# Two-expert feed-forward with cross attention: tiles turned in 16-bit halves, per-group statistics moved to GpSimd, new instruction orders

## The chip, the cores and the metric

The kernel runs on one core of one Trainium2 chip. The metric is the device time of one execution in microseconds, the median of several. A core has five engines that work side by side, each through its own instruction list in order: TensorE (PE, with weight loads shown as PEld), VectorE (DVE), ScalarE (ACT), GpSimd (POOL) and SyncE (SP), which only issues transfers here. They wait for one another through semaphores.

## What is computed

`x` and `ctx_1024` hold 128 sequences of 64 tokens with 128 features, all in float32. Cut to what matters, the reference is:

```python
def attn(query, kv):                       # causal, one head, per sequence
    scores = einsum('bqd,bkd->bqk', query, kv) * 128 ** -0.5
    scores = where(tril, scores, -inf)
    return einsum('bqk,bkd->bqd', softmax(scores), kv)

x = x + attn(layernorm(x), ctx_1024)
xt = layernorm(x).reshape(-1, 128)         # 8192 tokens
logits = xt @ gate_w.T                     # 8 experts
_, idx = top_k(logits + beta, 2)
c = zeros(B, 8).at[rows, idx].add(sigmoid(logits[idx]))
h = silu(xt @ gate_proj[e]) * (xt @ up_proj[e])     # every expert e, width 256
combined = sum_e c[:, e] * (h @ down_proj[e])
shared = (silu(xt @ shared_gate) * (xt @ shared_up)) @ shared_down
x = x + combined + shared
```

## The kernel before

**Two stages.** The first takes the 8192 tokens in 16 groups of 512 (`G = 16`, four tokens to each of the 128 partitions, `GT = 4`). It does the attention, the routing and the shared expert, writes `x + attention + shared` to the output, and scatters each token's normalised row (128 features, token number, two expert numbers, two weights: `ROW = 133` float32) to a place in the DRAM array `sorted_rows` that depends on its pair of experts. The second stage reads this array back in 91 tiles of 128 rows (64 regular ones, and 27 with what the lists left over, which are taken two at a time), so 78 steps (`PAIRS`) of one or two tiles; a step multiplies its tiles with the two experts' weights and adds the result to the output through an indirect DMA.

**A group in the first stage.** VectorE takes mean and variance of the incoming tokens (`statistics(g, 0)`, line 873) and, from the attention's result, of the second layer norm (`statistics(g, 1)`). Both share one small computation for index j (first norm of group j, second of group j - 3; `LEAD = 3`): VectorE adds epsilon (`variances`, line 902), GpSimd raises to the power -1/2 (`powers`, line 441), and VectorE multiplies mean and result to a shift (`shifts`, line 907). The first norm itself is written by GpSimd for two of the four tokens (`normalise_x`, line 448; VectorE's `normalise_first` does it for the first four groups) and by ScalarE for the other two (`shift_x`, line 668). TensorE turns the result (line 1433), ScalarE copies it, TensorE adds mask and scores (lines 1440 and 1448), VectorE takes the row maximum (`row_max`, line 915), ScalarE the exponentials, TensorE the attention (`attend`, line 1473), VectorE the residual (`residual`, line 930). Then `normalise` on ScalarE (line 659), `transpose_xn2` (line 1485), `route` (line 1493) and `turn_logits` (line 1499) on TensorE, `bias_logits` and `choose` on VectorE (lines 941 to 974: the two experts and a one-hot row `chosen` of the pair), `pick` on GpSimd (line 465: the logits' tanh at the chosen experts), `weights` on VectorE (line 983), `ranks` on TensorE (lines 1508 to 1514: the token's place in its pair's list) and `slots` on VectorE (lines 988 to 995), and at last four indirect DMAs of `scatter` on GpSimd (line 478). The shared expert is `shared_gate_mm` and `shared_up_mm` (lines 1527 and 1536, 512 columns each), `silu_gates`, `hidden` (line 1002), `shared_down_mm` (line 1548) and `sum_up` (line 1008).

**Order.** All five lists are written out by hand: a prologue, a loop over pairs of groups, and an epilogue. Each engine obeys its own list, so an instruction that waits holds everything behind it. SP loads `x` into a ring of five buffers (`RX = 5`): `load_x(5)` is the first that waits, for `residual(0)`, and it stands behind the 2.1 MB that fill `sorted_rows` with padding and behind `load_c(4)` and `load_c(5)`.

**From the first stage to the second.** `tile_table` and `slot_tables` on VectorE (lines 1030 to 1066) work out where each tile lies and which experts it needs; TensorE's `list_ends` and `spread_table` (lines 1555 and 1560) stand in its list between the last shared matrix products. After `shared_down_mm(15)` TensorE does eight products that keep it busy (line 1822), and then turns the first tiles.

**A step of the second stage** is in TensorE's list: `gate_up(i)` (line 1609; 8 products of 128x128x128 in float32, which the profile shows as 16 instructions), `transpose_tile(i + 2)` (line 1575, one instruction for each tile, into PSUM bank G0 or U0), `tile_down(i - 1)` (line 1633, 8 instructions). VectorE's list for it: `tile_hidden(i)` (line 1171), `copy_tile_T(i + 2)` (line 1121, from PSUM to SBUF), `tile_weights(i + 1)`, `tile_out(i - 1)`; in steps 0 to 7 the tables for the left-over rows (`left_table`, `extra_table`) come on top.

## Time and profile before

| | |
|---|---|
| median of 3 runs | 396.43 us (396.29 to 396.6) |
| the profiled execution, its own time | 396.57 us |
| its span | 394.9 us |
| TensorE busy | 379.7 us, 96% |
| VectorE busy | 294.4 us, 75% |
| ScalarE busy | 236.2 us, 60% |
| GpSimd busy | 251.0 us, 64% |
| first matrix product of the second stage | at 169.98 us |

The profiled execution's own time is 0.14 us over the median, and 1.67 us longer than its span. Times of the trace count from the span's start. Matrix instructions are pipelined, so the busy time of a short stretch of TensorE contains their overlap; the distance from one start to the next tells what each costs. The granted clock was 0.996 of full speed over the span.

### The profile page before, as it was taken

The numbers are of one execution on the slowest core, as the hardware profiler recorded it, in microseconds if no ns is written. First come the engines' busy times: TensorE is split into PE (matmuls) and PEld (weight loads), VectorE is DVE, ScalarE is ACT, GpSimd is POOL, SyncE is SP. The second block draws the span as 40 slices with busy tenths as digits, with TensorE's granted clock in tenths as the row PEclk, the third lists the DMA queues.
The fourth block names the chain that finished last, engine by engine and source line by source line (L and its number), as shares of the span: only waits on it lengthen the run. The fifth ranks groups of instructions, "written<-read, shape, count | busy, mean of one in ns | idle before, by whom it ended". The sixth has DMA issues, their size and how long they took to land.

```text
span 394.9 us, 11090 instructions
## 1 busy us (share of the span) xinstructions
PE 379.7 (96%) x3321; PEld 318.3 (81%) x3321; DVE 294.4 (75%) x1308; ACT 236.2 (60%) x558; POOL 251.0 (64%) x275
## 2 busy tenths in 40 slices
PE   8979999999999999899999999999999999999993
PEld 3445666666666665689999999999999999999993
DVE  4988989999998896687966666667677666666662
ACT  2689898798888863355566565652211565656540
POOL 6636888888877787338787788886100045645464
PEclk9999999999999999999999999999999999999998
DMA  7953464896442112247556775554332113332223
GB/s 239 354 165 103 141 210 136 253 280 199 136 149 83 64 62 77 70 120 143 104 86 91 87 100 77 72 81 59 59 74 55 36 21 54 45 48 23 26 22 27
DMA packets 43049, 41.78 MB, mean 106 GB/s; under 512 B 5688, under 2 KB 31808, under 8 KB 42992
## 3 DMA queue, kind: packets, MB, share of 16 engines
q1 hardware_dynamic: 30864, 30.69, 26.8%
q0 software_dynamic: 12128, 10.40, 19.1%
q8 instruction: 28, 0.46, 0.5%
q14 instruction: 29, 0.24, 0.2%
HBM read 24.17 MB, written 16.90 MB: 104 GB/s over the span
## 4 chain that ended last, share of the span: by engine, by line
PE 57%; POOL 1%; issue 1%; DVE 1%; ACT 0%; POOLq 0%; DVEq 0%
PE gu_pair L1609 35%; PE bank L1633 17%; PE bank L1575 2%; PE bank L1548 1%; POOL out L529 1%; PE bank L1536 0%; PE gu_pair L1822 0%; POOL sorted_rows L478 0%; PE bank L1527 0%; DVE acc L1008 0%; PE gu_pair L1560 0%; DVE hid L1002 0%; ACT tile_T L727 0%; DVE t_out L1211 0%; DVE t_part L1205 0%
## 5 line engine op out<-in xcount | busy, mean ns | idle before, releaser
L529 POOL DMA_INDIRECT out<-t_out,tile_in x64 | 100.2, 1565 | 85.0 <-DVE t_out L1211 70.6
L1609 PE MATMUL gu_pair<-tile_T,W_slot 128*128 128x128 f32 x1024 | 124.8, 275 | 0.5 <-ACT tile_T L727 0.5
L1609 PEld LDWEIGHTS gu_pair<-tile_T,W_slot 128*128 128x128 f32 x1024 | 119.5, 192 | 0.7 <-issue 0.7
L756 ACT ACTIVATE t_silu<-gu_pair 128x512 f32<-128x512 f32 (+1 forms) x78 | 46.4, 594 | 101.8 <-PE gu_pair L1609 94.8
L1171 DVE SCALAR_TENSOR_TENSOR t_hid<-t_silu,gu_pair 128x512 f32<-128x512 f32 (+1 forms) x78 | 53.1, 680 | 48.4 <-PE gu_pair L1609 47.2
L1633 PE MATMUL bank<-W_down,t_hid 128*128 (+1 forms) x620 | 82.3, 276 | 0.1
L478 POOL DMA_INDIRECT sorted_rows<-rows,slot x64 | 63.4, 990 | 20.5 <-issue 20.0
L1633 PEld LDWEIGHTS bank<-W_down,t_hid 128*128 128x128 f32 x620 | 75.4, 192 | 0.7 <-issue 0.7
L746 ACT ACTIVATE W_slot<-W 128x512 f32 x128 | 73.2, 622 | 3.9 <-DVE slot_pair L1062 2.0
L489 POOL DMA_INDIRECT left_in<-sorted_rows,left_index x27 | 26.1, 967 | 16.8 <-DVE left_index L1089 8.9
L441 POOL TENSOR_TENSOR rstd<-var_eps,minus_half 128x8 f32<-128x8 f32 (+1 forms) x19 | 27.9, 1470 | 10.9 <-DVE var_eps L902 10.5
L1536 PE MATMUL bank<-xn_T,shared_gu 128*128 128x512 f32 x64 | 33.9, 611 | 0.6 <-ACT silu_g L723 0.6
L1548 PEld LDWEIGHTS bank<-shared_dn,hid 128*128 128x128 f32 x256 | 29.9, 192 | 5.0 <-issue 4.5
L1548 PE MATMUL bank<-shared_dn,hid 128*128 128x128 f32 x256 | 31.9, 278 | 1.5 <-issue 0.9
L1527 PE MATMUL bank<-xn_T,shared_gu 128*128 128x512 f32 x64 | 33.0, 603 | 0.0
L659 ACT ACTIVATE rows<-x,shift,rstd 128x128 f32<-128x128 f32 x64 | 26.3, 485 | 3.4 <-DVE shift L907 3.3
L1609 PE MATMUL gu_pair<-tile_T,W 128*128 128x128 f32 x216 | 26.4, 275 | 0.0
L1609 PEld LDWEIGHTS gu_pair<-tile_T,W 128*128 128x128 f32 x216 | 25.2, 192 | 0.0
L1211 DVE SCALAR_TENSOR_TENSOR t_out<-bank,t_weight,t_part 128x128 f32<-128x128 f32 x64 | 22.5, 351 | 2.3
L1121 DVE COPY tile_T<-bank 128x128 f32<-128x128 f32 (+1 forms) x76 | 23.3, 306 | 0.0
L1002 DVE TENSOR_TENSOR hid<-silu_g,bank 128x512 f32<-128x512 f32 x32 | 21.6, 677 | 2.2 <-ACT silu_g L723 1.6
L1575 PE MATMUL bank<-ident,tile_in 128*128 128x128 f32 x91 | 22.5, 273 | 0.0
(158 smaller groups left out, 543.5 us busy)
## 6 DMA issues: line engine op xcount, KB each, us to landing
tile_in<-sorted_rows SPq DMA_DIRECT2D x91, 66.5 KB, 2.0
x_sb<-x SPq DMA_DIRECT2D x16, 256.0 KB, 4.4
c_T<-ctx_cols SPq DMA_DIRECT2D x16, 256.0 KB, 3.1
c_sb<-ctx SPq DMA_DIRECT2D x16, 256.0 KB, 4.6
out<-acc SPq DMA_DIRECT2D x16, 256.0 KB
sorted_rows<-padding SPq DMA_DIRECT2D x1, 2128.0 KB, 12.7
sorted_rows<-left_in SPq DMA_DIRECT2D x27, 66.5 KB, 2.4
sorted_rows<-rows,slot POOLq DMA_INDIRECT x64, 3.1
```

The source lines that it names most:

```text
L441: e.tensor_tensor(rstd[:, j % 2, n], var_eps[:, n], minus_half[:, n], ALU.pow).then_inc(s_rstd, 1)
L478: e.indirect_dma_start(sorted_rows, bass.IndirectOffsetOnAxis(ap=slot[:, g % RR, i:i + 1], axis=0), rows[:, g % RR, i, :], None).then_inc( ...
L529: e.indirect_dma_start(out_flat, bass.IndirectOffsetOnAxis(ap=tile_in[:, tiles_of(i)[0] % NR, ID:ID + 1].bitcast(I32), axis=0), t_out[:, q ...
L746: r = e.activation(W_slot[:, q % TX, h], W[:, bass.ds(experts[q][h] * WN, WN)], ACT.Copy)
L756: e.activation(t_silu[:, 0:n * M], gate_up_pair[i % 2][0][:, 0:n * M], ACT.Silu).then_inc(s_t_silu, 1)
L1171: e.scalar_tensor_tensor(out=t_hid[:, i % 2, 0:n * M], in0=t_silu[:, 0:n * M], scalar=0.5, in1=gate_up_pair[i % 2][1][:, 0:n * M], op0=ALU ...
L1527: e.matmul((G0, G1)[m], shared_gu[:, 0, m * P:(m + 1) * P], xn2_T[:, g % RT], start=True, stop=True).then_inc(s_gate[m], 1)
L1536: e.matmul((U0, G0)[m], shared_gu[:, 1, m * P:(m + 1) * P], xn2_T[:, g % RT], start=True, stop=True).then_inc(s_up[m], 1)
L1548: r = e.matmul(Y[:, i * D:(i + 1) * D], hid[:, g % 2, m, i * P:(i + 1) * P], shared_dn[:, m], start=(m == 0), stop=(m == MC - 1), skip_gro ...
L1575: r = e.transpose(tile_pair[i % 2][:, h * P:(h + 1) * P], tile_in[:, n % NR, 0:D], ident[:])
L1609: r = e.matmul(bank[:, c:c + P], w, tile_T[:, i % TX, tile], start=True, stop=True, skip_group_check=True)
L1633: r = e.matmul(y, t_hid[:, i % 2, c:c + P], w, start=(m == 0), stop=(m == MC - 1), skip_group_check=True)
```

## The change

It has six parts.

1. From step 2 of the second stage on, each tile is turned as two matrices of 16-bit numbers: the low and the high halves of the float32 words, each read with a step of two 16-bit elements, each turned against a bfloat16 identity. `copy_tile_T` then puts the halves together again, as 16-bit integers, 256 of them for each tile in place of 128 float32.
2. `variances` and `shifts` go from VectorE to GpSimd; there the negated mean is a separate instruction.
3. From group 4 on GpSimd normalises one token in four, and ScalarE three.
4. `scatter` is split in two halves, which stand apart in GpSimd's list.
5. `pick` for groups 13 to 15 is done by VectorE (`pick_late`).
6. The lists of all five engines get a new order.

```diff
@@ sync_program
             load_x(0)
-            load_c(0)
             load_x(1)
             e.dma_start(router[:], gate_w).then_inc(s_router_in, 16)
+            load_c(0)
+            load_x(2)
             load_c(1)
-            load_x(2)
+            load_x(3)
             e.dma_start(beta_all[:], ...
             load_c(2)
-            load_x(3)
@@ gpsimd_program
+            def variances(j):
+                n = norms(j)
+                if j < G:
+                    e.wait_ge(s_moments[0], j + 1)
+                if j >= LEAD:
+                    e.wait_ge(s_moments[1], j - LEAD + 1)
+                if j:
+                    e.wait_ge(s_shift, j)
+                    e.wait_ge(s_rstd, j)
+                e.tensor_scalar(minus_mean[:, n], moments[:, j % 2, n, :, 0], -1.0, None, ALU.mult).then_inc(s_minus_mean, 1)
+                e.tensor_scalar(var_eps[:, n], moments[:, j % 2, n, :, 1], EPS, None, ALU.add).then_inc(s_var_eps, 1)
...
+            def shifts(j):
+                n = norms(j)
+                e.wait_ge(s_minus_mean, j + 1)
+                e.wait_ge(s_rstd, j + 1)
+                e.tensor_tensor(shift[:, j % 2, n], minus_mean[:, n], rstd[:, j % 2, n], ALU.mult).then_inc(s_shift, 1)
...
-                for i in range(GT // 2):
-                    r = e.tensor_scalar(xn[:, i], x_sb[:, g % RX, i], moments[:, g % 2, 0, i, 0:1],
-                                        rstd[:, g % 2, 0, i:i + 1], ALU.subtract, ALU.mult)
-                r.then_inc(s_normal[0], 1)
+                e.tensor_scalar(xn[:, 0], x_sb[:, g % RX, 0], moments[:, g % 2, 0, 0, 0:1],
+                                rstd[:, g % 2, 0, 0:1], ALU.subtract, ALU.mult).then_inc(s_normal[0], 1)
...
-                for i in range(GT):
+                for i in range(half * GT // 2, (half + 1) * GT // 2):
                     e.indirect_dma_start(
                         sorted_rows, bass.IndirectOffsetOnAxis(ap=slot[:, g % RR, i:i + 1], axis=0),
@@ scalar_program, shift_x
-                for i in range(GT // 2, GT):
+                for i in range(GT // 2 if g < FIRST else 1, GT):
@@ vector_program
+            def pick_late(g):
+                e.wait_ge(s_is_chosen, g + 1)
+                e.wait_ge(s_tanh, g + 1)
+                e.wait_ge(s_weights, g)
+                e.tensor_tensor(picked[:, :, :, 0:E], is_chosen[:, :, :, :],
+                                tanh_l[:, :, :].rearrange("p t (a e) -> p t a e", a=1).broadcast_to([P, GT, K, E]),
+                                ALU.mult).then_inc(s_picked, 1)
@@ copy_tile_T
-                e.tensor_copy(tile_T[:, i % TX, 0:n].rearrange("p h n -> p (h n)"), tile_pair[i % 2][:, 0:n * P]).then_inc(s_tile_T, 1)
+                e.tensor_copy(tile_T[:, i % TX, 0:n].bitcast(U16).rearrange("p h (n c) -> p h c n", c=2),
+                              tile_halves[i % 2][:, 0:n * 2 * P].bitcast(U16).rearrange("p (h c n) -> p h c n", h=n, c=2)
+                              ).then_inc(s_tile_T, 1)
@@ vector_program, the part of its order between residual(1) and residual(2)
             residual(1)
             statistics(1, 1)
-            variances(4)
-            pair_tables()
             row_max(2)
             normalise_first(3)
-            shifts(4)
+            statistics(5, 0)
+            inverse_sums(2)
             bias_logits(0)
             choose(0)
-            statistics(5, 0)
             slots(0)
             weights(0)
-            inverse_sums(2)
             row_max(3)
             residual(2)
@@ vector_program, its order from choose(14) on
             choose(14)
+            pick_late(14)
+            weights(14)
             sum_up(12)
+            slots(14)
+            hidden(13, 1)
             hidden(13, 0)
-            slots(14)
-            weights(14)
-            hidden(13, 1)
             bias_logits(15)
             choose(15)
+            pick_late(15)
+            weights(15)
             slots(15)
             hidden(14, 0)
-            weights(15)
-            sum_up(13)
             hidden(14, 1)
             tile_table()
-            sum_up(14)
+            sum_up(13)
             hidden(15, 0)
             slot_tables()
+            sum_up(14)
             hidden(15, 1)
@@ transpose_tile
-                    r = e.transpose(tile_pair[i % 2][:, h * P:(h + 1) * P], tile_in[:, n % NR, 0:D], ident[:])
+                    if i < 2:
+                        r = e.transpose(tile_pair[i][:, 0:P], tile_in[:, n % NR, 0:D], ident[:])
+                        continue
+
+                    halves = tile_in[:, n % NR, 0:D].bitcast(BF16).rearrange("p (d c) -> p d c", c=2)
+                    for c in range(2):
+                        r = e.transpose(tile_halves[i % 2][:, (2 * h + c) * P:(2 * h + c + 1) * P], halves[:, :, c], ident_bf[:])
@@ tensor_program, its order from transpose_probs(2) to attend(2)
-            shared_gate_mm(0, 1)
+            shared_gate_mm(0, 0)
             turn_logits(0)
             transpose_probs(2)
             transpose_xn(3)
+            shared_gate_mm(0, 1)
+            transpose_xn2(1)
             ranks(0)
-            transpose_xn2(1)
             mask_scores(3)
             score(3)
             attend(2)
@@ tensor_program, its order from ranks(15) on
             ranks(15)
+            shared_up_mm(14, 1)
+            list_ends()
             shared_down_mm(13)
-            shared_up_mm(14, 1)
+            shared_up_mm(15, 0)
+            shared_gate_mm(15, 0)
             shared_gate_mm(15, 1)
-            list_ends()
+            spread_table()
             shared_down_mm(14)
-            shared_gate_mm(15, 0)
-            shared_up_mm(15, 0)
-            spread_table()
             shared_up_mm(15, 1)
             shared_down_mm(15)
```

The new lists for the groups between are of the same kind: the same calls, in another order.

## Rows read from the trace of the kernel before

**Rows 1.** Busy time by stretch: stretch, length, then each engine's busy us (instructions)

```profile
80.00:100.00 20.00, 20.00 (x203) 13.14 (x202) 19.08 (x103) 17.29 (x49) 17.10 (x21) 1.00 0.73 225
190.00:200.00 10.00, 9.98 (x87) 9.56 (x86) 8.92 (x26) 6.17 (x12) 7.89 (x7) 1.00 0.46 92
250.00:280.00 30.00, 30.00 (x272) 30.00 (x271) 19.77 (x63) 12.95 (x24) 21.95 (x15) 1.00 0.51 67
```

**Rows 2.** Chain that ended last, second stage: start us, length us, what

```profile
253.50 1.78 PE gu_pair L1609 x16
255.28 0.11 PE bank L1575
255.39 0.89 PE bank L1633 x8
```

**Rows 3.** Timeline of PE, one group of the first stage: start us, us, what

```profile
86.81 1.02 PE L1536 MATMUL bank<-xn_T,shared_gu 128*128 128x512 f32 x2
87.67 0.21 PE L1508 MATMUL gu_pair<-chosen,before_bf 128*128 128x112 bf16 x1
87.72 0.24 PE L1511 MATMUL gu_pair<-chosen,steps_bf 128*128 128x84 bf16 x3
87.81 0.46 PE L1514 MATMUL gu_pair<-list_next,last_row 128*128 128x112 f32 x2
88.11 0.27 PE L1440 MATMUL gu_pair<-mask,ident_bf 128*128 128x256 bf16 x1
88.22 1.02 PE L1527 MATMUL bank<-xn_T,shared_gu 128*128 128x512 f32 x2
89.17 0.67 PE L1473 MATMUL gu_pair<-c_sb,probs_T 64*64 64x128 f32 x16
```

**Rows 4.** Groups by line and shape: count, busy us, mean ns, idle before

```profile
L1609 PEld LDWEIGHTS gu_pair<-tile_T,W_slot 128*128 128x128 f32 x1024 | 119.5, 192 | 0.7 <-issue 0.7
L1121 DVE COPY tile_T<-bank 128x128 f32<-128x128 f32 x63 | 17.9, 283 | 0.0
L1121 DVE COPY tile_T<-bank 128x256 f32<-128x256 f32 x13 | 5.4, 418 | 0.0
L902 DVE TENSOR_SCALAR var_eps<-moments 128x8 f32<-128x8 f32 x13 | 2.7, 205 | 0.7
L907 DVE SCALAR_TENSOR_TENSOR shift<-moments,rstd 128x8 f32<-128x8 f32 x13 | 2.1, 162 | 0.7 <-POOL rstd L441 0.6
L448 POOL TENSOR_SCALAR xn<-x_sb,moments,rstd 128x128 f32<-128x128 f32 x24 | 18.9, 791 | 1.1 <-PE gu_pair L1433 0.3 <-POOL rstd L441 0.2
```

**Rows 5.** Timeline of DVE, prologue, and chosen of groups 2 and 11

```profile
23.34 0.19 DVE L941 TENSOR_TENSOR biased<-gu_pair,beta_all 128x32 f32<-128x32 f32 x1
25.07 0.27 DVE L974 TENSOR_TENSOR chosen<-pair_code,code 128x112 bf16<-128x112 f32 x1
26.55 0.87 DVE L873 BATCH_NORM_STATS2 stats<-x_sb 128x6 f32<-128x128 f32 x4 [1.21 <-DMA x_sb<-x]
...
42.36 0.27 DVE L974 TENSOR_TENSOR chosen<-pair_code,code 128x112 bf16<-128x112 f32 x1
...
123.44 0.27 DVE L974 TENSOR_TENSOR chosen<-pair_code,code 128x112 bf16<-128x112 f32 x1
```

**Rows 6.** Timeline of SP, prologue: issue of x, group 5; page, median to landing

```profile
19.01 0.43 SPq L323 DMA_DIRECT2D x_sb<-x  x1
...
x_sb<-x SPq DMA_DIRECT2D x16, 256.0 KB, 4.4
```

**Rows 7.** Timeline of the end of the first stage, all engines

```profile
154.18 0.27 DVE L974 TENSOR_TENSOR chosen<-pair_code,code 128x112 bf16<-128x112 f32 x1
157.52 0.33 POOL L465 TENSOR_TENSOR picked<-is_chosen,tanh_l 128x64 f32<-128x64 f32 x1
157.88 0.23 DVE L983 TENSOR_REDUCE rows<-picked 128x8 f32<-128x72 f32 x1 [1.47 <-POOL picked L465]
165.55 2.02 PE L1548 MATMUL bank<-shared_dn,hid 128*128 128x128 f32 x16 [0.88 <-issue]
```

598 lines of the change are left out of this document (353 added, 245 removed).

## Prediction

> **What bounds the kernel now.** I read the chain that ended last first. In the second stage it is TensorE alone: a step is 16 instructions of gate and up, one turned tile, 8 instructions of down, and the next step starts where the last one ends [rows 2]. 1.78 us for 16 and 0.89 us for 8 is 0.111 us each; a turned tile costs 0.11 us, the same. So whatever changes a step on TensorE changes the time, some 76 times over, and what VectorE does is beside the path as long as it keeps its lead. The busy time by stretch shows that lead: between 250 and 280 us VectorE is busy for 19.77 us of 30, TensorE for all of it [rows 1].
>
> For the first stage the busy table shows TensorE at 20.0 us of 20 and VectorE at 19.08 [rows 1], but a short product's busy time contains its neighbours, so I take starts. From choosing group 2 to choosing group 11, 42.36 to 123.44 us, nine groups take 9.0 us each [rows 5]. What a group costs TensorE I add up from start to start in the timeline [rows 3]: a pair of 512-column instructions 0.86 (86.81 to 87.67), four pairs 3.4; ranks 0.44 (87.67 to 88.11); attention some 0.6, and as much for the scores, which are as many instructions; the 16 instructions of down 1.78, as for 16 of gate and up [rows 2]; turning both norms, the probabilities and the logits eleven times 0.11; routing and mask, two short runs, some 0.5. The sum is about 8.6 us (3.4 + 0.4 + 1.2 + 1.8 + 1.2 + 0.5). VectorE's share of 19.08 in 20 is 8.6 us of a 9.0 us group. So both engines are within 0.4 us of the period, and neither can be relieved by more than that without the other being late next.
>
> **Tiles in halves, on TensorE.** 76 of the 78 steps change. A tile's one instruction of 0.11 us goes. In its place come two bfloat16 instructions of 128 columns. The nearest row is the 112-column bfloat16 product, which hands over after 0.05 us (87.67 to 87.72) [rows 3]; for 128 columns that is 0.056, and two make 0.112. The streaming is a wash. What is not a wash is the weight load behind them. A float32 load takes 192 ns from start to end and comes at TensorE's pace of 0.111 us [rows 2, 4], hidden because a product just as long runs ahead of it. In the changed step the first float32 load of the down product has only 0.056 us of bfloat16 work to hide in. The trace has this case once a group: two float32 products of 112 columns behind a bfloat16 product of 28 columns take 0.30 us, 87.81 to 88.11, where two at the steady pace take 0.22 [rows 3]. That is 0.08 us lost behind a product of some 0.03 us. Where the product ahead is as long as the load (0.11 us) nothing is lost. Between the two, at 0.056, the loss is 0.05 on a line and 0.04 if the load has a fixed length; I take 0.045. It comes once a step, with one tile or two: 76 x 0.045 = **+3.4 us**, bounds 0 and 76 x 0.08 = 6.1.
>
> The trace shows no weight load with a step between elements. If it doesn't get the short bfloat16 load but moves at the pace of the float32 load, each half costs 0.11: then 62 steps of one tile gain 0.11 us and 14 steps of two tiles 0.22, together 6.8 + 3.1 = +9.9 us. I take the short load as likelier, because the bfloat16 products of the ranks hand over in 0.05 us and less [rows 3], so a bfloat16 load is no brake there. The lower end is that nothing is lost; below that I see no way, since streaming alone is already even.
>
> A rule of the Trainium skill speaks against this part too: "TensorE: Matmul & The Clock Gate", section "Back-to-back issue gap", puts a stream of load-and-product pairs at about 81 ns each for 128 columns. The rows here disagree for short bfloat16 products (0.05 us and less [rows 3]). By the page two halves would take 0.162 us in place of 0.111, which is 89 tiles x 0.05 = +4.5 us, an estimate from that page.
>
> **Putting the halves together, on VectorE.** One tile's copy goes from 128 to 256 elements, read from PSUM and written with a step; the row of 256 elements is 418 ns against 283 [rows 4]. That is +0.135 us in 62 steps, and by the same slope +0.27 us in 14 steps: 12 us of VectorE. It lies beside TensorE's work: a step of 2.79 us has about 0.95 us of VectorE idle (10.2 of 30 us [rows 1]). Only while the tables for the left-over rows are made is the cover thin: 8.92 of 10 us busy between 190 and 200 us [rows 1]. Some seven steps there, each 0.135 longer, against 1.1 us idle in 10: I add 0.3 us, bounds 0 and 1. If the cover were gone everywhere, it would be up to 12 us, but the idle time is three to seven times the addition.
>
> Second stage: 3.4 + 0.3 = **+3.7 us**.
>
> **Prologue.** This is an order that can be read. VectorE's new list has `statistics(5, 0)` ahead of `bias_logits(0)` and `choose(0)`; before, it stood behind. In the trace choosing ran from 23.34 to 25.34 us, and only then did VectorE wait, until 26.55 us, for x of group 5 [rows 5]. That load was issued at 19.01 us [rows 6], behind the padding, c of group 4 and c of group 5, which the change leaves ahead of it. It took 7.5 us, 19.01 to 26.55, where the median load of x takes 4.4 [rows 6], so it hangs on the bytes ahead, and an earlier issue would not help much. I keep its landing near 26.5. Then VectorE does the statistics (1.25 us), and choosing (2.0 us) begins near 27.9 and ends near 29.9, 4.6 us later than before. Queued behind it: `slots(0)`, `row_max(3)`, `residual(2)`; on TensorE `ranks(0)` with the scores of group 3 and attention of group 2 behind. Since VectorE only swapped two items of 1.25 and 2.0 us around a wait, what it is late by afterwards is the 2.0 us of choosing that it could have done before the landing: **+2.2 us** with the small operations. Bounds: 0, if x lands by 23.3, and 4.6.
>
> **Steady groups.** `variances` and `shifts` leave VectorE: 0.205 + 0.162 = 0.37 us for each group [rows 4]. GpSimd gains three small instructions for them. Its nearest prices are 0.33 us for 64 elements on each of 128 partitions [rows 7] as an upper end, and nothing beyond issue as a lower, so 0.3 to 1.0 us; it loses one normalised token of 0.79 [rows 4]. It was busy for 17.10 of 20 us [rows 1] and stays about there. ScalarE gains that token: by its own share of 17.29 in 20 it has 1.2 us idle in a group, and the token takes it about half a microsecond. Both stay off the path, but ScalarE now runs near 90%. The gain on the path is not 0.37: TensorE's sum of 8.6 allows at most 0.4 before it is the one that is late, and both engines would need perfect order. I take half, 0.2 us for each of 11 groups: **-2.2 us**, bounds 0 and -4.4.
>
> **Scatters by halves** change no count; their only customers are the ring of seven row buffers and the second stage's start, so I cost them at nothing.
>
> **End of the first stage.** Before, VectorE waited 1.47 us for GpSimd's pick of group 15, which stood behind scatters [rows 7]. `pick_late` takes that wait away, for three instructions of at most 0.33 us [rows 7]. What is late next is TensorE's own list. From the end of choosing group 15 (154.45) to `shared_down_mm(15)` at 165.55 are 11.1 us [rows 7]. In the new order `slot_tables` still stands behind `hidden(15, 0)`, which needs both gate products of group 15 and their silu, and `hidden(15, 1)` behind that. So the chain from choosing on keeps its members; only the picking leaves it, and other products now come between. I take **-0.3 us**; the bounds are +1, the three instructions on VectorE with nothing hidden, and -2, the wait and a little more.
>
> **Sum.** 396.57 (the profiled execution) + 3.7 + 2.2 - 2.2 - 0.3 = 400.0 us. That execution is 0.14 us over the median of the runs, so 399.8.
>
> **Rivals.** First, *the new orders fill TensorE's gaps*. It has 9.0 against 8.6 us in each group, and more in the prologue. If the orders win back 4 us over the groups, 1.5 us at the end, and x of group 5 lands before VectorE asks for it, the sum is 396.4 + 3.7 - 5.5 = 394.6, faster. It decides from 4.5 us won in the first stage on. For it: VectorE's relief is real, 0.37 us a group. Against: 8.6 us leaves no room for more, and the swap above. 0.18.
>
> Second, *turning in halves costs nothing*, because the first float32 load is hidden some other way: 399.8 - 3.4 = 396.4, no change. For it: the streaming is even. Against: the 0.30 us of two float32 products [rows 3]. 0.14.
>
> Third, *the stepped load is slow*: 399.8 - 3.4 + 9.9 = 406.3. For it: no such load in the trace. 0.12.
>
> Fourth, *the prologue's loss is not won back*, since ScalarE at 90% or GpSimd's longer chain (mean, variance, power, shift, between scatters) holds the groups at 9.0 us: 399.8 + 2.2 = 402.0. 0.14.
>
> The forecast has 0.42 and its own range 398 to 401.5.
>
> **How the numbers follow.** A measurement of this kernel tells about 0.2% (0.8 us) from no change. Faster by more: 0.14 of the first rival, 0.05 of the second, 0.01 of the forecast, and some for a mix of the first two: 0.23. Within 0.2%: 0.04 of the first, 0.09 of the second, 0.01: 0.14. Slower: 0.63. The range for 8 in 10 leaves out a third of the first rival below, half of the third above: 394.0 to 406.0.
>
> **What would show it.** In the chain after: the distance from the end of gate and up to the down product, 0.11 before, should be about 0.11 with the down product's 8 instructions taking 0.93 to 0.95 in place of 0.89, so a step of 2.83 us; 2.79 means the second rival, 2.9 the third. VectorE's wait for x of group 5 should stand ahead of choosing group 0, at about 26.5 us, and choosing end near 30. The period of groups 2 to 11 should be 8.8 us; at 8.65 the first rival is at work, at 9.0 the fourth. The first product of the second stage should start near 169.7 us (169.98 before). The prediction is wrong if the turned halves take another time than the rows of bfloat16 products give, or if x of group 5 comes early.

## The result: 23 us slower, and where they are

The changed kernel takes 419.86 us (median of 4 runs, 419.59 to 420.61), the kernel before, run beside it, 396.51 (396.29 to 396.92). The ratio is 1.0591 (1.0572 to 1.0609), so +23.4 us where 3.3 were forecast. The profiled execution took 420.07 us with a span of 418.3.

Where the time lies can be read from a few starts that both traces have: the one-hot row `chosen` of groups 0, 2, 11 and 15, and the first product of the second stage. Before, they stand at 25.07, 42.36 and 123.44 [rows 5], 154.18 [rows 7] and 169.98. After, first in the timeline of DVE (start us, us, what):

```profile
26.78 0.87 DVE L988 BATCH_NORM_STATS2 stats<-x_sb 128x6 f32<-128x128 f32 x4 [4.63 <-DMA x_sb<-x]
...
29.75 0.27 DVE L1073 TENSOR_TENSOR chosen<-pair_code,code 128x112 bf16<-128x112 f32 x1
...
45.94 0.27 DVE L1073 TENSOR_TENSOR chosen<-pair_code,code 128x112 bf16<-128x112 f32 x1
...
138.09 0.27 DVE L1073 TENSOR_TENSOR chosen<-pair_code,code 128x112 bf16<-128x112 f32 x1
...
172.36 0.27 DVE L1073 TENSOR_TENSOR chosen<-pair_code,code 128x112 bf16<-128x112 f32 x1
172.72 0.23 DVE L1083 TENSOR_TENSOR picked<-is_chosen,tanh_l 128x64 f32<-128x64 f32 x1
```

and in that of PE:

```profile
187.38 1.80 PE L1722 MATMUL gu_pair<-tile_T,W_slot 128*128 128x128 f32 x14 [0.46 <-ACT tile_T L806]
```

| stretch | before | after | difference | forecast |
|---|---|---|---|---|
| start to `chosen` of group 2 | 42.36 | 45.94 | +3.6 | +2.2 |
| group 2 to group 11 | 81.08 (9.0 a group) | 92.15 (10.2) | +11.1 | -1.8 (8.8) |
| group 11 to group 15 | 30.74 | 34.27 | +3.5 | -0.4 |
| group 15 to the second stage | 15.80 | 15.02 | -0.8 | -0.3 |
| second stage | 224.9 | 230.9 | +6.0 | +3.7 |

The fourth column adds up to 23.4. Most of it is in the groups, where the forecast had a small gain. There TensorE and VectorE are no longer nearly full, as the busy time by stretch shows (columns as in [rows 1], whose first row had TensorE at 20.00 and VectorE at 19.08):

```profile
80.00:100.00 20.00, 18.97 (x175) 12.15 (x177) 17.35 (x95) 16.40 (x47) 15.48 (x23) 1.00 0.79 251
100.00:120.00 20.00, 17.50 (x158) 11.26 (x150) 14.58 (x86) 16.10 (x47) 15.00 (x23) 1.00 0.50 149
120.00:140.00 20.00, 18.81 (x169) 12.99 (x170) 17.32 (x99) 15.76 (x46) 13.50 (x21) 0.91 0.31 97
```

So they wait. For what, the table of waits says (engine and line, what it waited for: us in total, times, longest). Before:

```profile
PEld gu_pair L1508 <- DVE chosen L974: 6.3, 13, 0.8
DVE stats L873 <- DMA x_sb<-x: 3.6, 2, 2.4
ACT rows L659 <- DVE shift L907: 3.3, 7, 1.1
```

After:

```profile
DVE stats L988 <- DMA x_sb<-x: 17.9, 9, 4.6
PEld gu_pair L1615 <- DVE chosen L1073: 13.7, 12, 3.8
ACT rows L738 <- POOL shift L464: 11.3, 11, 1.5
```

Two waits at the head of a chain are new in size: VectorE for x, 17.9 us where it was 3.6, and ScalarE for a shift, 11.3 where it was 3.3. (TensorE's wait for `chosen`, 13.7 where it was 6.3, follows from the first: in the next section it falls to 5.2 as soon as x is on time.) The first has its reason in two lists read side by side. SP's queue and VectorE, after, at group 8 (start us, us, what):

```profile
51.38 0.33 SPq L333 DMA_DIRECT2D c_T<-ctx_cols  x1
51.75 1.00 SPq L334 DMA_DIRECT2D c_sb<-ctx  x1
52.79 0.44 SPq L328 DMA_DIRECT2D x_sb<-x  x1
```

```profile
53.51 0.38 DVE L996 BATCH_NORM_AGGREGATE moments<-stats 128x2 f32<-128x6 f32 x4
57.67 0.87 DVE L988 BATCH_NORM_STATS2 stats<-x_sb 128x6 f32<-128x128 f32 x4 [3.78 <-DMA x_sb<-x]
...
60.57 0.27 DVE L1073 TENSOR_TENSOR chosen<-pair_code,code 128x112 bf16<-128x112 f32 x1
```

SP holds `load_x(8)` behind `load_c(8)`, and `load_c(8)` waits for group 4's attention, since c has a ring of four buffers (`RC = 4`). The new list of VectorE has `statistics(8, 0)` directly behind `residual(4)` and `statistics(4, 1)`, so VectorE asks for x of group 8 at 53.9 us, 1.1 us after its transfer was issued, and the transfer takes more than 4. VectorE sits idle for 3.78 us, with `choose(3)` queued behind. Before, the same statistics stood behind `residual(5)`, one group later, and its x had been issued 9.5 us earlier:

```profile
47.92 0.43 SPq L323 DMA_DIRECT2D x_sb<-x  x1
...
57.39 0.86 DVE L873 BATCH_NORM_STATS2 stats<-x_sb 128x6 f32<-128x128 f32 x4
```

So the new list asks for x four groups ahead of the residual where the old one, in its loop, asked three ahead, and SP's list, which is the same in its loop, lets x of four groups ahead start only about when that residual does. In the loop `statistics(g + 9, 0)` stands likewise behind `residual(g + 5)`, with `statistics(g + 5, 1)` and `row_max(g + 6)` between. Of the 17.9 us of such waits 9.9 are in the groups, six waits of 0.4 to 3.8 us (x of groups 6, 8, 11, 13, 14 and 15); before, there was none in the groups, and all 3.6 us were in the prologue.

### The profile page after: what moved, and what is told of

Read it like the earlier page. It is cut to its first block, busy times and chain, and to the rows that moved or that the text cites. A ratio compares the mean times of both kernels' runs of the same rounds, so it can differ in the third digit from the quotient of the medians.

```text
span 418.3 us, 11327 instructions
## 1 busy us (share of the span) xinstructions
PE 389.2 (93%) x3414; PEld 325.3 (78%) x3414; DVE 303.8 (73%) x1273; ACT 240.6 (58%) x570; POOL 255.8 (61%) x317
## 4 chain that ended last, share of the span: by engine, by line
PE 54%; DVE 4%; POOL 2%; issue 2%; ACT 1%; DVEq 0%; POOLq 0%; ACTq 0%
PE gu_pair L1722 30%; PE bank L1746 16%; PE bank L1688 2%; PE bank L1655 2%; PE bank L1634 1%; POOL sorted_rows L499 1%; PE bank L1643 1%; DVE extra_sum L1286 1%; ACT rows L738 1%; POOL out L550 1%; DVE t_hid L1281 1%; DVE tile_T L1229 1%; PE gu_pair L1964 0%; DVE t_out L1321 0%; DVE t_part L1313 0%
## 5 line engine op out<-in xcount | busy, mean ns | idle before, releaser
L1746 PE MATMUL bank<-W_down,t_hid 128*128 (+1 forms) x620 | 86.3, 282 | 1.5 <-DVE t_hid L1281 1.3
L499 POOL DMA_INDIRECT sorted_rows<-rows,slot x64 | 64.7, 1010 | 24.6 <-issue 21.8
L1229 DVE COPY tile_T<-bank 128x256 uint16<-128x256 uint16 (+1 forms) x76 | 37.2, 490 | 0.0
L738 ACT ACTIVATE rows<-x,shift,rstd 128x128 f32<-128x128 f32 x64 | 26.3, 484 | 11.3 <-POOL shift L464 11.3
L988 DVE BATCH_NORM_STATS2 stats<-x_sb 128x6 f32<-128x128 f32 x64 | 13.9, 280 | 18.0 <-DMA x_sb<-x 17.9
```

Of the source, the lines that this page charges most:

```text
L499: e.indirect_dma_start(sorted_rows, bass.IndirectOffsetOnAxis(ap=slot[:, g % RR, i:i + 1], axis=0), rows[:, g % RR, i, :], None).then_inc( ...
L738: r = e.activation(rows[:, g % RR, i, 0:D], x2[:, g % RG, i], ACT.Identity, bias=shift[:, (g + LEAD) % 2, 1, i:i + 1], scale=rstd[:, (g + ...
L1229: e.tensor_copy(tile_T[:, i % TX, 0:n].bitcast(U16).rearrange("p h (n c) -> p h c n", c=2), tile_halves[i % 2][:, 0:n * 2 * P].bitcast(U16 ...
L1746: r = e.matmul(y, t_hid[:, i % 2, c:c + P], w, start=(m == 0), stop=(m == MC - 1), skip_group_check=True)
```

## Experiments

All are runs of whole kernels, each compared with the kernel before on the same chip (medians 396.3 to 397.4 us, with one exception, which is named). Starts and waits of a kernel come from its one profiled execution. Where a difference between two kernels is given, it is the difference of their ratios times 396.5.

### Late x: mended in the changed kernel, and made in the kernel before

**x ahead of c** (changed kernel). Theory: the late x is most of the loss.

```diff
             for it in range(2, G + 3):
-                if it + 3 < G:
-                    load_c(it + 3)
                 if it + 3 < G:
                     load_x(it + 3)
+                if it + 3 < G:
+                    load_c(it + 3)
```

> The changed kernel with one edit: in SP's loop the load of x for a group stands ahead of the load of c for it, so it waits only for the residual five groups back and no longer for the attention four groups back. In the changed kernel VectorE waits 17.9 us in total for x, nine times, and the nine groups from choosing group 2 to choosing group 11 take 10.2 us each. Theory (late x): the waits for x from group 6 on vanish, the period falls to 9.2 us or less and the time to about 409 us (419.9 less 11). Rival (GpSimd's chain of mean, variance, power and shift holds the groups, and VectorE would wait for something else): the waits for x vanish too, but the period stays above 10 us and the time above 417 us. Second rival (the lower granted clock of TensorE in three stretches is the cause and not a result): time above 417 us and the clock still falls.

Measured: 411.03 us, ratio 1.0371 (1.0346 to 1.0396). That is 8.7 us less than the changed kernel. The waits for x fall from 17.9 to 7.4 us, three in the prologue, the longest of them, 3.9, for group 5; in the groups none is left.

Groups 2 to 11 go from 10.2 to 9.3 us each (`chosen` at 45.16 and 128.87), not to 9.0.

**x one turn later** (kernel before). The opposite test: nothing of the change but a late x.

```diff
-                if it + 3 < G:
-                    load_x(it + 3)
+                if it == 2:
+                    load_x(5)
+                if 6 <= it + 2 < G:
+                    load_x(it + 2)
```

> The kernel before with one edit: from group 6 on SP issues the load of x one turn of its loop later, so behind the load of c of the next group. This gives the kernel before the distance of the changed one: the load is issued after the attention whose residual stands just ahead of the statistics that read it. Theory (late x is what lengthens the period): VectorE waits some 2 us for x in each group, the period grows from 9.0 to about 10.5 us and the time to about 410 us. Rival (VectorE's wait is filled from slack and the period is set elsewhere): at most 399 us.

Measured: 431.53 us, 1.0891 (1.0857 to 1.0926), +35 us, far more than expected. VectorE's waits for x:

```profile
DVE stats L875 <- DMA x_sb<-x: 32.9, 12, 6.8
```

29.3 us more of waiting (32.9 against 3.6) cost 35 us, and in the run above 10.5 us less gave back 8.7. Part of the 35 is TensorE's clock: granted at 0.967 over the span where the kernel before has 0.996, which is at most some 13 us. That leaves 22 to 35 us for the 29.3. So a wait of VectorE ahead of choosing costs most of its length or all of it: little of it is covered by other work, and the chain through choosing sets the period.

**x ahead of c in the kernel before**, the same diff as the first, on a kernel whose VectorE waits only 3.6 us for x.

> The kernel before with one swap on SP's list: in the loop x of a group is loaded ahead of its c. Its VectorE waited only 3.6 us for x, twice. If a late x costs what it waits, 2 to 3 us less: 394 (393 to 395.5). If the old order has room to hide it, no change: 396.4. A loss would mean that the c that is now later is what attention waits for.

Measured: 395.64 us, 0.9969 (0.9959 to 0.998), -1.2 us. The swap moves the issue of `load_x(5)` from 19.0 to 15.5 us, and the waits for x go from 3.6 to 2.0. The traces don't show that the gain comes from there: the kernel with halves alone (below) has SP's old order, waits 2.4 us for x in its profiled execution and chooses group 15 at 153.42 us, and this one at 153.46. The expected 2 to 3 us would have needed the whole wait gone.

### The prologue

**statistics(5, 0) behind choosing**, on top of x ahead of c (changed kernel).

```diff
-            statistics(5, 0)
             inverse_sums(2)
             bias_logits(0)
             choose(0)
+            statistics(5, 0)
```

It ran first, with three of the kernels of the next sections, at a time when the kernel before itself took 459.7 us, for a reason that the runs don't show. The ratios of then (0.9641 for this one; 0.995, 1.0057 and 1.0103 for part 2, part 3 and part 5 alone) are used for nothing, and all four were run again beside a kernel before of 397.4 us.

> The changed kernel with x ahead of c in SP's loop, as in the run e1_x_ahead_of_c (411.0 us), and also the statistics of group 5 behind choosing group 0, as before. In e1 VectorE still waits 3.9 us at once for x of group 5 and chooses group 0 at 29.0 us (25.1 in the kernel before). Theory (that wait holds choosing, and what it costs is what VectorE could have done before the landing, 2.0 us): choosing group 0 ends near 26 us, choosing group 2 comes near 43 us in place of 45.2, and the time is 409 us. Rival (the delay is given back later anyway, since other chains hold the groups): 411 us, no change.

> The kernel of e5_x_ahead_stats_behind again, since in that job the kernel before took 459.7 us in place of 396.5 and everything waited longer. The changed kernel with x ahead of c in SP's loop and the statistics of group 5 behind choosing group 0. Theory (the wait for x of group 5 costs the 2 us of choosing that could be done before): 409 us where e1_x_ahead_of_c took 411.0. Rival (given back later by other chains): 411 us.

Measured: 408.04 us, 1.028 (1.0258 to 1.0301), 3.6 us less than with x ahead of c alone by the ratios, 3.0 by the times. `chosen` of group 0 starts at 26.04 in place of 28.97, and the 3 us stay with it to the end. The wait itself explains these 2.9 us. With it went a stretch of low clock: from 28 to 36 us the granted clock was 0.58 with the wait, and the mean of the span rose from 0.989 to 0.995, so some of the 3.6 can be clock. Groups 2 to 11 still take 9.3 us each.

### Turned halves

**Float32 turns in the changed kernel** and **halves alone in the kernel before**: part 1 taken out of the one and put into the other (the two hunks of `copy_tile_T` and `transpose_tile` of the diff above, backwards and forwards).

> The changed kernel with its tiles turned and copied as float32, as before; all else of the change stays. The step of the second stage is 2.79 us again in place of 2.845, and the stalls near 200 us and between 310 and 340 us go. Theory (each step loses one float32 weight load behind a short product, 0.055 us, 76 times, and VectorE's longer copies 1.8 us): 419.9 - 6 = 413.9 us. Rival (the copies cost nothing of their own; the 1.8 us come from the new order): 419.9 - 4.2 = 415.7 us. Rival (the halves cost nothing): 419.9 us.

> The kernel before with only part 1 of the change: tiles from step 2 on turned in halves and copied as 16-bit integers. Theory (0.055 us of TensorE a step, 76 steps, and 1.8 us of stalls behind VectorE's copies): 396.5 + 6 = 402.5 us. Rival (only TensorE's part): 400.7 us. The forecast's own size for this part was 3.7 us: 400.2 us.

Measured: without the halves 413.57 us, 1.0433 (1.0407 to 1.0458), so they cost 6.3 us of the change; alone 402.55 us, 1.0159 (1.0133 to 1.0185), +6.3 us. The two agree, and a third pair below gives 6.1. This part stands by itself. Its costs are seen in the chain of the second stage, after (start us, length us, what; before [rows 2]):

```profile
252.95 1.79 PE gu_pair L1722 x16
254.74 0.11 PE bank L1688 x2
254.85 0.95 PE bank L1746 x8
```

and in the groups by shape (count, busy us, mean ns; before [rows 4]):

```profile
L1688 PEld LDWEIGHTS bank<-ident_bf,tile_in 128*128 128x128 bf16 x178 | 16.5, 99 | 0.8
L1229 DVE COPY tile_T<-bank 128x256 uint16<-128x256 uint16 x63 | 27.7, 440 | 0.0
L1229 DVE COPY tile_T<-bank 128x512 uint16<-128x512 uint16 x13 | 9.5, 729 | 0.0
```

Two halves take the 0.11 us of the one tile; the down product behind them takes 0.95 in place of 0.89. With finer digits the first float32 product of down starts 0.056 us after the second half, and the next one 0.165 after it, 0.055 over the pace of 0.111: 76 x 0.055 = 4.2 us. Of the other 1.8 us, 1.1 lie in one place. In the chain after:

```profile
325.53 1.79 PE gu_pair L1722 x16
327.31 0.13 PE bank L1688 x2
327.44 0.71 DVE tile_T L1229
...
330.05 0.45 DVE tile_T L1229
...
332.79 0.69 DVE t_hid L1281
...
333.52 1.16 PE bank L1746 x8
```

From 327 to 333 us the chain leaves TensorE and runs over VectorE. These are the last steps with two tiles, where VectorE has the copy of 512 elements (0.73 us, 0.42 before) and a row of `extra_sum` instructions that wait for one another. TensorE is idle for 1.1 us of 300 to 340 (38.91 of 40 busy; 40 of 40 before). Another 0.4 us is idle from 200 to 220, where the tables for the left-over rows are made (19.62 of 20). In the kernel with halves alone the first of these places (299 to 316 us there) costs 1.2 us, and the second, 190 to 200 us, 0.1; so 0.3 us of the 1.8 has no place.

### Mean, variance and shift on GpSimd

**Part 2 alone** in the kernel before:

```diff
@@ gpsimd_program, around each powers(j)
+            variances(j)
             powers(j)
+            shifts(j)
@@ vector_program
-            variances(j)
-            shifts(j)
```

> The kernel before with only part 2 of the change: variances and shifts on GpSimd, each around its power, in GpSimd's list of before. Theory A (the move costs the groups: GpSimd reaches these instructions late, between scatters, so ScalarE waits for the shift; in e1_x_ahead_of_c ScalarE waits 14.3 us for it, 3.3 before): VectorE is relieved by 0.37 us a group, yet the period grows from 9.0 to 9.2 or more and the time to 399 us or more. Theory B (the relief decides, as the forecast had it): the period falls to 8.8 and the time to 394.5 us. Theory C (nothing on the path): 396.3 us within 0.8.

> The kernel of e6_before_var_on_gpsimd again: the kernel before with variances and shifts on GpSimd. Theory A (ScalarE waits longer for the shift and the groups take more than 9.0 us): 399 us or more. Theory B (VectorE's relief of 0.37 us a group decides): 394.5 us. Theory C (nothing on the path): 396.5 us within 0.8.

Measured: 411.31 us, 1.0362 (1.034 to 1.0383), **+14 us** for three small instructions that were forecast at nothing. Groups 2 to 11 take 10.0 us each, those from 11 to 15 take 36.1 us where it was 30.7. The waits, and GpSimd's timeline:

```profile
ACT rows L708 <- POOL shift L460: 19.5, 14, 3.1
PEld gu_pair L1488 <- ACT rows L708: 14.6, 13, 2.0
```

```profile
62.43 0.25 POOL L442 TENSOR_SCALAR minus_mean<-moments 128x8 f32<-128x8 f32 x1
62.76 0.25 POOL L443 TENSOR_SCALAR var_eps<-moments 128x8 f32<-128x8 f32 x1
63.09 1.67 POOL L454 TENSOR_TENSOR rstd<-var_eps,minus_half 128x8 f32<-128x8 f32 x1
64.90 0.20 POOL L460 TENSOR_TENSOR shift<-minus_mean,rstd 128x8 f32<-128x8 f32 x1
...
...
71.09 0.95 POOL L497 DMA_INDIRECT sorted_rows<-rows,slot  x1 [0.30 <-issue]
...
72.31 0.25 POOL L442 TENSOR_SCALAR minus_mean<-moments 128x8 f32<-128x8 f32 x1
```

In the kernel before, the same stretch of GpSimd's list, and what GpSimd waited for from 60 to 120 us (the largest row; the other two are 0.3 and 0.2 us):

```profile
59.07 1.67 POOL L441 TENSOR_TENSOR rstd<-var_eps,minus_half 128x8 f32<-128x8 f32 x1
...
67.88 1.70 POOL L441 TENSOR_TENSOR rstd<-var_eps,minus_half 128x8 f32<-128x8 f32 x1
```

```profile
POOL sorted_rows L478 <- issue: 7.7, 28, 0.3
```

GpSimd's list was already full. From one power to the next it takes 8.81 us, and in these 60 us GpSimd waited for other engines for 0.5 us only; the 7.7 us before the scatters are time in which it waited for nothing that the profile shows. They aren't counted as busy, so 84 us of 100 (40 to 140 us) looked like room. A scatter is busy for 0.96 us and takes 1.26 from start to start. With the three instructions the list takes 9.88 us for a group (62.43 to 72.31), and from 60 to 120 us GpSimd waits for no other engine at all:

```profile
POOL sorted_rows L497 <- issue: 6.9, 25, 0.3
```

That is the new period of 10.0 us. The instructions are small (0.20 to 0.25 us each), but from start to start they add 0.33 + 0.33 + 0.2 us to a list without room, and ScalarE's wait for the shift (19.5 us in all) and TensorE's for ScalarE's rows follow. This is read from the two traces. No run gives the list room in the old order with the three instructions in it (part 2 with part 3), which would test it.

**Part 2 taken out of the changed kernel** (with x ahead of c and statistics behind choosing). This was the theory for what is left after late x, prologue and halves.

```diff
@@ vector_program, the same at every group
             statistics(g + 4, 1)
+            variances(g + 7)
             bias_logits(g + 3)
             choose(g + 3)
+            shifts(g + 7)
@@ gpsimd_program
-            variances(j)
             powers(j)
-            shifts(j)
```

> The changed kernel with x loaded ahead of c, statistics(5, 0) behind choosing (as in the run at 408.0 us) and, new, variances and shifts back on VectorE, one instruction each, variances behind the second norm's statistics and shifts behind the next choosing. Theory A, GpSimd's chain of mean, variance, power and shift is what is left: ScalarE's 14.4 us of waiting for a shift of GpSimd mostly goes, the period of groups 2 to 11 falls from 9.3 to 9.0 or below, 403.0 us (402 to 404.5), 5 us less. Rival B, the new orders of VectorE and TensorE themselves cost it (a product of another group stands in a worse place): the time stays at 407 to 409 and the wait is only renamed.

Measured: 408.55 us, 1.03 (1.0285 to 1.0314), no gain at all; the theory falls. Groups 2 to 11 take 9.3 us each as before the edit. Only the ends shift: `chosen` of group 0 comes 2.1 us later (28.2) and the stretch from group 11 to the second stage is 2.1 us shorter. So with the new orders the move to GpSimd costs nothing and brings nothing on the whole, and in the old order it costs 14 us. In the changed kernel GpSimd has lost one token of 0.80 us in each group to ScalarE (part 3), about what it gains; with the move its list takes 9.0 us (105.73 to 114.72 us of the kernel of 408.04 us, no wait between), without it GpSimd has waits of its own again (6.5 us for `var_eps` from 40 to 140 us), and the period doesn't fall. So at 9.3 us something else in the new orders holds it as well. ScalarE's wait for the shift is only renamed, as rival B said: 14.4 us for GpSimd's before this edit, 12.2 for VectorE's after it.

### ScalarE's third token and the late picks

**Part 3 alone** and **part 5 alone**, in the kernel before:

```diff
@@ shift_x, and normalise_x correspondingly with one token
-                for i in range(GT // 2, GT):
+                for i in range(GT // 2 if g < FIRST else 1, GT):
```

```diff
@@ vector_program, for groups 13, 14 and 15 (and out of GpSimd's list)
+            pick_late(15)
             weights(15)
```

> The kernel before with only part 3 of the change: from group 4 on ScalarE normalises three tokens in four and GpSimd one. Theory A (ScalarE at 86% of its time has no room on the chain from shift to turning, so the 0.48 us come onto the path in each of 12 groups): up to 5 us slower, 398 to 401 us. Theory B (GpSimd's 0.79 us less is worth as much): 396.3 us within 0.8. The forecast had it at nothing.

> The kernel of e7_before_three_on_scalar again: the kernel before with three tokens in four normalised on ScalarE from group 4 on. Theory A (ScalarE has no room on its chain): 398 to 401 us. Theory B (GpSimd's relief is worth as much): 396.5 us within 0.8.

> The kernel before with only part 5 of the change: the picks of groups 13 to 15 on VectorE, right ahead of the weights. VectorE no longer waits 1.47 us for GpSimd's pick of group 15. Theory A (what stands behind that wait on VectorE, the tables among it, is on the path into the second stage): 1.0 to 1.5 us faster, 395.0 us. Theory B (as the forecast had it, TensorE's own list and silu are late next): 396.3 less 0.3 us, no change that can be told.

> The kernel of e8_before_pick_late again: the kernel before with the picks of groups 13 to 15 on VectorE. Theory A (the wait taken away was on the path): 395.0 us. Theory B (others are late next): 396.2 us, no change that can be told.

Measured: 396.72 us, 0.998 (0.9966 to 0.9994), and 396.7 us, 0.999 (0.9977 to 1.0004). Neither costs anything; the first may bring a little. In the profile of the first, groups 2 to 11 take 8.94 us each in place of 9.01, and GpSimd waits again. In that of the second, the stretch from `chosen` of group 15 to the second stage is 15.1 us in place of 15.8, most of what the changed kernel gained there; the medians don't tell it from no change.

### The new orders by themselves

**The new orders alone**: the kernel of 408.55 us with float32 turns. What is left of the change is the orders, scatters by halves, ScalarE's third token and the late picks.

> The same with each tile turned as one float32 matrix again and copied as 128 float32: what is left of the change is the new orders, scatters by halves, three tokens on ScalarE and the late picks, with x ahead of c. If the accounts close (23.4 us = 6.2 turned halves + 8.8 late x + 3.0 prologue + some 5.4 GpSimd), this one is at 396.8 us (395.5 to 398.5), and 6.2 below the run above. If something of the orders costs or gains by itself, it shows here: 399 or more, or 394 or less.

Measured: 402.52 us, 1.0145 (1.0129 to 1.016), +5.7 us over the kernel before and 6.1 below the kernel with halves. So the orders cost 5.7 us by themselves, beyond the late x and the prologue's swap, and 7.0 against the kernel before with the same x ahead of c (0.9969). Busy time of 40 to 140 us, kernel before and this one:

```profile
40.00:140.00 100.00, 99.15 (x913) 65.44 (x912) 92.87 (x535) 85.22 (x248) 83.91 (x99) 1.00 0.51 162
```

```profile
40.00:140.00 100.00, 96.64 (x884) 64.29 (x880) 90.48 (x510) 86.54 (x249) 73.76 (x89) 1.00 0.49 155
```

TensorE is idle for 3.4 us of 100 where it was for 0.9, and the groups take 9.3 us in place of 9.0. The waits that grew (3.3 and 2.3 us before):

```profile
ACT rows L685 <- DVE shift L969: 12.2, 11, 2.0
PEld gu_pair L1614 <- ACT rows L685: 9.3, 9, 2.3
```

**The second norm's turning put back behind attention**, first in this kernel, then in the one of 408.04 us. The new list of TensorE has `transpose_xn2(g + 3)` ahead of the next group's scores and attention in every other group. The theory was that this wait is the 5.7 us.

```diff
                 ranks(g + 2)
-                transpose_xn2(g + 3)
                 mask_scores(g + 5)
                 score(g + 5)
                 attend(g + 4)
-                route(g + 3)
+                transpose_xn2(g + 3)
                 shared_gate_mm(g + 2, 0)
-                turn_logits(g + 3)
+                route(g + 3)
                 shared_down_mm(g + 1)
+                turn_logits(g + 3)
```

> The kernel of the new orders alone (402.5 us), with one thing of TensorE's order put back as it was before, in seven of the groups: the turning of the second norm stands behind the next group's scores and attention, a 512-column product stands between it and route, and the down product between route and turn_logits. In the kernel of the new orders TensorE waited 9.3 us of weight-load time, nine times, for ScalarE's normalised rows at that turning (before: 2.3 us, five times). Theory C, this wait is what the new orders cost: it falls to 3 us or less, the period of groups 2 to 11 from 9.3 to 9.1 or below, and the time to 398.5 (397 to 400). Rival D, the new order is slow in other places as well and the wait only moves to the next instruction: 401.5 to 403.

> The same edit in the changed kernel with x loaded ahead of c and statistics(5, 0) behind choosing (408.0 us), so with turned halves and with mean, variance, power and shift on GpSimd. Theory C: 4 us less there too, 404 (403 to 406). If GpSimd's longer chain makes the rows late whatever TensorE does meanwhile, less than 2 us is won: 406.5 to 408.

Measured: 410.66 us, 1.0341 (1.0321 to 1.0361), and 414.49 us, 1.0421 (1.0401 to 1.0442): 8 and 6 us slower, not 4 faster. The wait for the rows did fall, but another, 6.4 us before the edit, took its place:

```profile
PEld gu_pair L1614 <- ACT rows L685: 5.5, 4, 2.3
PEld gu_pair L1637 <- DVE chosen L1036: 10.0, 11, 2.1
```

The edit put a 512-column pair ahead of `route` and a down product ahead of `turn_logits`, so routing came later, and with it choosing and ranks; the groups take 10.0 us. Both outcomes that were written down were wrong. A smaller entry in the table of waits went with a longer time, so the size of a wait isn't the price of its cause. The reading, which no run shows by itself, is that the instruction that waited had room and the chain from the second norm to the ranks had none; the edit moved three things at once. Why the new orders cost 5.7 us stays open between their many swaps; where they cost them is known: 1.8 us up to `chosen` of group 2, 2.9 in groups 2 to 11, 1.5 up to group 15, 0.8 gained from there to the second stage, and 0.4 in the second stage.

### A version that beats both

**Before, with what cost nothing or gained**: x ahead of c, three tokens on ScalarE, three late picks.

> The kernel before with the three edits that cost nothing or gained alone: x ahead of c in SP's loop (395.6 alone against 396.8), three tokens on ScalarE (0.998) and the last three picks on VectorE (0.999). If the three add up, 395.0 (394.3 to 395.6), the fastest of all; if they relieve the same waits, 395.6 as the first alone.

Measured: 394.91 us (394.63 to 395.21), 0.9939 (0.9925 to 0.9953), 2.4 us below the kernel before and 26 below the changed one. Groups 2 to 11 take 8.94 us each.

## Why the prediction was wrong

The direction was right, the size wrong by a factor of seven. The account by the runs: halves 6.3, late x in the groups 8.7, the prologue's swap 3.6, together 18.6; the rest, 4.8, is what the new orders cost otherwise, and the kernel that has them nearly alone says 5.7.

**Steady groups, forecast -2.2 with 0 as its worst, measured +14.6: the step that failed.** It took VectorE's relief from `variances` and `shifts` as a gain and priced the new order at nothing, as "the same calls, in another order". By the runs the 14.6 are 8.4 of late x (groups 2 to 11 take 92.15 us with it, 83.71 without), 4.4 of the orders alone (2.9 and 1.5), and the rest, 1.8, shows only with the move to GpSimd, in groups 11 to 15. The prediction had done exactly the right reading for group 5: where `statistics(5, 0)` stands, when its x is issued, what is queued behind it. The same reading of `statistics(8, 0)`, and of the loop's `statistics(g + 9, 0)`, against SP's `load_c` ahead of `load_x` gives the late x. The numbers were there: attention of group 4 frees SP, x lands 4.4 us after its issue [rows 6], and VectorE asks for it after a residual and one set of statistics, some 2.5 us of work. That is about 2 us wherever the new list has nothing else between; after, the four largest such waits are 3.8, 1.4, 2.7 and 1.2 us.

**The balance argument was turned the wrong way round.** Both engines within 0.4 us of the period [rows 3, 5] was read as "no more than 0.4 to gain". It says as much that there is nothing to lose: every wait of either, if it stands on the chain through choosing, lengthens the period. The rivals and the lower half of the range were spent on gains that the same sum had excluded, while the upper end of the steady groups was 0. Where 96% of the period is work of either engine, a new order can win 4% at most and lose without such a bound, and the range should have been open to that side.

**The move to GpSimd, costed at nothing.** The balance for GpSimd, 0.3 to 1.0 us more against a token of 0.79 less, was right: by the groups of the trace after, the three instructions are 260 + 243 + 208 ns = 0.71 us. What it was set against was not. Busy for 17.10 of 20 us was read as room, but the time before each scatter isn't in it, and by starts GpSimd's list took 8.8 us of 9.0. With the change it takes 9.0 (as read above), so a period of 8.8, as forecast, was out of reach whatever VectorE gained. The fourth rival named GpSimd's longer chain, but let it hold the groups at 9.0 at the worst. In the old order, with two tokens left on GpSimd, the same three instructions cost 14 us. The busy share hides that too: 83.9 us of 100 before and 83.7 with the move, but over 9.0 us a group that is 7.6 us of work, and over 10.0 us it is 8.4.

**TensorE in the halves, forecast 3.4, measured 4.2.** The mechanism was right and so was its place. The term was 0.045 and is 0.055: with 0.056 us to hide in, the float32 load loses all of the rest of 0.111. The line drawn between the lossless case and the 0.08 us behind a 28-column product was a little low. (The prediction also counted 62 steps of one tile and 14 of two, where [rows 4] count 63 and 13; no sum moves by more than 0.1 us.) The Trainium skill, "TensorE: Matmul & The Clock Gate", section "Back-to-back issue gap", has 81 ns for a pair; this trace doesn't agree, its halves start 0.055 us apart, although that page's sum of +4.5 us lay close to the 4.2 for another reason. The rival with a slow stepped load is excluded: the load takes 99 ns.

**VectorE's copies, forecast 0.3, measured about 1.8.** The prices were nearly right (440 and 729 ns; 418 for the first had been taken). The cover was read from means: 19.77 of 30 us busy [rows 1] does not say that every step has a third of VectorE idle. The two-tile steps have a row of dependent instructions, in which VectorE idles and is late all the same. The chain before runs on TensorE alone there, so it showed no sign; what would have shown it is VectorE's timeline of one two-tile step, with its gaps behind `extra_sum`, set against a step of 2.9 us.

**Prologue, forecast +2.2.** Right in kind and in its landmarks: x of group 5 landed at 26.8 (26.5), choosing ended at 30.0 (29.9). With x ahead of c in the loop it was issued 3.7 us earlier (15.73 in place of 19.39) and landed at 26.0, so an earlier issue helped little, as was said. The part that isn't made up later was 3.0 to 3.6 us, some of it perhaps clock. **End of the first stage, -0.3:** -0.8 from `chosen` of group 15 to the second stage, inside its bounds; `pick_late` starts 0.36 us behind `chosen`, and the wait of 1.47 us [rows 7] is gone. **ScalarE's third token and scatters:** nothing, as forecast for the first; the second has no run of its own.

Of the landmarks that were to decide, the period did: 10.2 us, beyond the 9.0 of the worst rival. The step of the second stage, 2.85 us by the chain, lies beside the 2.83 that was written down.

## What to carry to other kernels

When a change reorders lists, redo for the loop body the reading that one does for the prologue: for each instruction that consumes a transfer, find what releases the transfer's issue, add the landing time, and compare it with the time at which the consumer now stands in its list. When two engines are both near the period, a wait on the chain between them costs most of its length or all of it, and the range has to be open to the slow side. Busy shares tell neither: VectorE with a third of its time free still had a stretch where a longer copy was late, and GpSimd, busy for 84%, had no room for three instructions of 0.2 us. Whether an engine is full is read from start to start of the same instruction in two groups, and from what the engine waited for: if that is almost nothing, its list sets the period or is about to.

## What the runs showed of the hardware

**TensorE's clock after a wait.** Behind the three longest waits for x (4.63, 3.78 and 2.71 us) the granted clock fell as well. The stretch around one of them (columns as above; the number ahead of the DMA share is the granted clock):

```profile
58.00:60.00 2.00, 0.00 (x0) 0.00 (x0) 1.93 (x21) 0.94 (x4) 1.41 (x2) 1.00 0.10 34
60.00:61.00 1.00, 0.10 (x2) 0.11 (x3) 0.93 (x6) 1.00 (x4) 0.26 (x1) 0.94 0.21 68
61.00:62.00 1.00, 1.00 (x8) 1.00 (x8) 1.00 (x3) 0.06 (x1) 0.86 (x2) 0.50 0.03 8
65.00:66.00 1.00, 1.00 (x10) 0.16 (x9) 0.97 (x5) 0.25 (x1) 0.69 (x2) 1.00 0.25 33
```

TensorE idled from 57.97 to 60.90, waiting for `chosen`, which waited for x; ahead of the other two falls it had idled for 2.75 and 2.28 us. It then ran at 0.50, its lower level of 1.2 GHz, until between 64 and 65 us; the four turned tiles of the second norm took 1.06 us in place of 0.60 to 0.66. So part of a late transfer's price can be paid in clock: the mean over the span fell from 0.996 to 0.985, and rose to 0.989 with x ahead of c. From these means, 0.015 of 418.3 us less 0.004 of 394.9 is 4.7 us, about the most that the clock can have cost of the 23.4.

**Bfloat16 weights read with a step of two elements load as fast as packed ones:** 99 ns against 96 to 99 for those of `ranks` in the trace before. **A float32 weight load behind two short bfloat16 products costs 0.055 us** at a pace of 0.111. **An indirect DMA on GpSimd occupies more of its list than its busy time:** 0.96 us busy, 1.26 us from start to start in the scatters. **16-bit integer copies from PSUM** that interleave halves take 440 ns for 256 elements and 729 for 512, the slope of float32 copies of as many elements and no faster: (729 - 440) / 256 = 1.13 ns an element, against (418 - 283) / 128 = 1.05 [rows 4].
